# Three of four first normalizations move from ahead of the distance attention into its first units

## What is computed

```
x = x + _L0_attn_ref(_layernorm(x, axis=-1), W_in, b_in, W_out, b_out)

P = X @ W_in + b_in                      # per head: Q, K, V, G of 64 columns each
W = power(1e-4 + cdist(Q, K), -2)        # cdist: root of q2 + k2 - 2 q k
W = W / (1e-4 + sum(W, axis=-1))
H = G * (W @ V)                          # gate times weighted values
return H @ W_out + b_out
```

## Time and profile before

| | us |
|---|---|
| median of 3 runs | 1476.16 (1475.1 to 1477.63) |
| span of the profiled execution | 1475.0 |
| TensorE busy | 1314.3 (89%) |
| VectorE busy | 1067.5 (72%) |
| ScalarE busy | 970.3 (66%) |
| GpSimd busy | 398.6 (27%) |

### The profile page before, as it was taken

One profiled execution on the slowest core, in us unless ns is written; L12 is line 12 of the kernel. 1 busy time (PEld: TensorE's weight loads), 2 busy tenths in 40 slices (PEclk: granted clock), 3 DMA queues, 4 the chain that ended last, 5 costly groups with the idle time before them and its releaser, 6 DMA issues.

```text
span 1475.0 us, 17072 instructions
## 1 busy us (share of the span) xinstructions
PE 1314.3 (89%) x6134; PEld 718.5 (49%) x6134; DVE 1067.5 (72%) x1814; ACT 970.3 (66%) x1264; POOL 398.6 (27%) x262
## 2 busy tenths in 40 slices
PE   6999998999899999567989898899989999986666
PEld 3444454445444544332323232477756767763344
DVE  7788858885888588168988898346548677658895
ACT  4999978997899789334777777445545454433321
POOL 1445533553355335410000000023310000006333
PEclk9999999999999999868999999999989999998887
DMA  8100000000000001000000000000010000000000
GB/s 183 42 1 1 0 1 1 0 1 1 0 1 0 0 1 56 17 1 0 1 0 1 0 1 1 1 1 1 1 54 1 1 1 1 1 1 1 0 8 22
DMA packets 27711, 15.01 MB, mean 10 GB/s; under 512 B 16638, under 2 KB 26476, under 8 KB 27500
## 3 DMA queue, kind: packets, MB, share of 16 engines
q1 hardware_dynamic: 27628, 13.92, 3.5%
HBM read 12.87 MB, written 1.05 MB: 9 GB/s over the span
## 4 chain that ended last, share of the span: by engine, by line
PE 34%; issue 24%; POOL 20%; DVE 18%; ACT 2%; DMA 0%; POOLq 0%; SPq 0%; ACTq 0%; DVEq 0%
POOL ARENA L2134 10%; DVE ARENA L880 9%; POOL ARENA L2139 6%; PE PS L1055 4%; PE PS L729 4%; PE PS L712 4%; PE PS L636 3%; POOL ARENA L2146 3%; PE PS L1063 2%; PE PS L1086 2%; PE PS L1078 2%; PE PS L1067 2%; PE PS L1740 1%; DVE Y L1973 1%; PE PS L1106 1%
## 5 line engine op out<-in xcount | busy, mean ns | idle before, releaser
L1740 PE MATMUL PS<-ARENA 128*128 128x512 f32 x512 | 227.3, 597 | 7.5 <-issue 6.7
L2031 DVE TENSOR_SCALAR ARENA<-PS,ARENA 128x512 f32<-128x512 f32 x256 | 188.1, 748 | 27.6 <-PE PS L1740 9.9
L2134 POOL TENSOR_TENSOR ARENA<-ARENA 128x1024 f32<-128x1024 f32 x64 | 151.3, 2365 | 132.5 <-ACT ARENA L1884 127.5
L880 DVE TENSOR_REDUCE ARENA<-PS 128x2 f32<-128x1024 f32 x128 | 146.4, 1214 | 13.3 <-PE PS L604 12.0
L1740 PEld LDWEIGHTS PS<-ARENA 128*128 128x128 f32 x512 | 95.3, 191 | 117.3 <-issue 113.4
L1868 ACT ACTIVATE ARENA<-ARENA 128x2048 f32<-128x2048 f32 x64 | 119.7, 1905 | 47.6 <-DVE ARENA L2031 47.3
L790 ACT ACTIVATE ARENA<-PS 128x1024 f32<-128x1024 f32 x128 | 128.3, 1025 | 32.4 <-PE PS L623 24.6
L1014 POOL TENSOR_TENSOR ARENA<-ARENA 128x512 f32<-128x512 f32 x32 | 40.6, 1270 | 390.5 <-DVE ARENA L994 390.3
L1876 ACT ACTIVATE ARENA<-ARENA,consts_sb 128x2048 f32<-128x2048 f32 x64 | 127.8, 1996 | 0.4
L1749 PE MATMUL PS<-ARENA 128*64 128x512 f32 x512 | 119.8, 611 | 8.1 <-ACT ARENA L1884 8.1
L1884 ACT ACTIVATE ARENA<-ARENA 128x2048 f32<-128x2048 f32 x64 | 118.3, 1897 | 0.0
(11 more groups left out here) (258 smaller groups left out, 2522.6 us busy)
## 6 DMA issues: line engine op xcount, KB each, us to landing
ARENA<-in_window_bias_dram SPq DMA_DIRECT2D x1, 1536.0 KB, 6.7
WKVG<-in_L_attn_W_in_dram SPq DMA_DIRECT2D x3, 448.0 KB, 6.9
X<-in_x_dram SPq DMA_DIRECT2D x4, 256.0 KB, 5.5
W<-in_L_ffn_w_dram SPq DMA_DIRECT2D x1, 1024.0 KB
out_dram<-X SPq DMA_DIRECT2D x4, 256.0 KB, 2.3
WQ<-in_L_attn_W_in_dram SPq DMA_DIRECT2D x2, 448.0 KB, 8.0
BV<-in_L_attn_b_in_dram SPq DMA_DIRECT2D x1, 512.0 KB, 6.3
Wout<-in_L_attn_W_out_dram SPq DMA_DIRECT2D x1, 512.0 KB, 5.1
```

Of the source, the lines that this page charges most:

```text
L880: dve.tensor_reduce(NMX[:, w % 2, t, 2 * jp:2 * jp + 2], bank(("cS", w, i)), AX.X, ALU.max, negate=True).then_inc(sem("c_max"), 1)
L1740: done(pe.matmul(o, SK[:, hd, kt * P:(kt + 1) * P], MQ[:, hd, :], start=True, stop=True), ("S", u, c))
L2031: dve.tensor_scalar(D[:, u % 2, hd, kt, :], bank(("S", u, c)), K2[:, u % 2, kt, hd:hd + 1], 1e-30, ALU.add, ALU.max).then_inc(sem("guarded ...
L2134: pool.tensor_tensor(WPAIR, D[:, u % 2, hd, 0:2], D[:, u % 2, hd, 2:4], ALU.add).then_inc(sem("w_paired"), 1)
```

## The change

Ahead of the loop only batch 0 is normalized, transposed and copied out. In the loop, `stats(0, u+1)` on VectorE and `rstd(0, u+1)` on ScalarE come in unit `u` (0 to 2); `normalize(0, u)` on VectorE, `ln_turn(0, u)` on TensorE and `xt_out(0, u)` on ScalarE in unit `u` (1 to 3). On VectorE they stand behind the key norms of the unit, on TensorE between its key norms and the next unit's scores, on ScalarE behind the exponentials. GpSimd adds the output bias to batch `u` behind `sum_weights(u)` in units 0 to 3, and no longer waits for its own four additions. The order in which PSUM banks are handed out changes accordingly.

```
 def psum_jobs():
-    jobs = [(("ln", 0, b), 1, [("xt_ready", b + 1)]) for b in range(B)]
+    jobs = [(("ln", 0, 0), 1, [("xt_ready", 1)])]
...
             jobs += project_queries(u + 1) + key_norms(u + 1)
+        if 1 <= u < B:
+            jobs += [(("ln", 0, u), 1, [("xt_ready", u + 1)])]
...
-            for b in range(B):
-                ln_turn(0, b)
+            ln_turn(0, 0)
...
                     key_norms(u + 1)
+                if 1 <= u < B:
+                    ln_turn(0, u)
...
-            for b in range(B):
-                rstd(0, b)
-            for b in range(B):
-                xt_out(0, b)
+            rstd(0, 0)
+            xt_out(0, 0)
...
                 weights(u)
+                if u + 1 < B:
+                    rstd(0, u + 1)
+                if 1 <= u < B:
+                    xt_out(0, u)
...
-            layernorm(0)
+            stats(0, 0)
+            normalize(0, 0)
...
                     key_norms(u + 1)
+                if u + 1 < B:
+                    stats(0, u + 1)
+                if 1 <= u < B:
+                    normalize(0, u)
...
-            for b in range(B):
+            def add_bias(b):
                 pool.wait_ge(sem("ln_y"), b + 1)
                 pool.tensor_tensor(X[:, b], X[:, b], Bout[:].unsqueeze(1).to_broadcast([P, QT, P]),
                                    ALU.add).then_inc(sem("x_biased"), 1)
-            pool.wait_ge(sem("x_biased"), B)
...
                 sum_weights(u)
+                if u < B:
+                    add_bias(u)
```

More of the change, by code:

```diff
@@ L1975, in normalize @@
                 ins.then_inc(sem("ln_y"), 1)
-            def layernorm(k):
-                for b in range(B):
[L1979 to L1982, removed]
             def evacuate_keys(u):
```

## The result

The changed kernel takes 1484.38 us (median of 4 runs, 1482.98 to 1484.99); the kernel before took 1475.63 beside it (1474.66 to 1477.63). The ratio is 1.0055 with a 95% interval of 1.004 to 1.0069: slower by 0.55%, 8.75 us in the medians (1483.4 was forecast, as 7.2 us on top of 1476.16). The profiled executions have spans of 1483.2 and 1475.0.

The account below looks back on a forecast made before the run. TensorE was taken as the loop's bound, without slack; head -4.3, waits 3.64 + 3.64 + 2.44 and clock +1.8 gave +7.2 us on 1476.16, so 1483.4 us. The 8-in-10 range was 1478.0 to 1488.0.

Parts of the forecast that it names:

- Head, -4.3: Before the loop: first scores at 19.2 instead of 23.49, BV's landing the last wait; gain 4.3 us, at least 3.5.
- Weights of the other heads stay covered: After the first scores: remaining weights land at 24.6, TensorE asks at 26.1, so that wait stays covered by 1.5 us.
- The wait in the loop, 3.64 + 3.64 + 2.44 = 9.7: Units 1 to 3: TensorE's transposes wait for VectorE's late normalization, costing 3.64, 3.64 and 2.44 us.
- The clock, +1.8: TensorE's scores after new idle time in units 1 and 2: one clock fall, 1.8 us, bounds 0 and 3.6.
- rival C: VectorE's loop work comes early enough to hide the wait: 1473.2, or 1472.4 without the earlier clock fall; chance 0.08.
- Sum: Whole kernel: -4.3 + 3.64 + 3.64 + 2.44 + 1.8 = +7.2 us, giving 1483.4 us, 0.5% slower.
- Nothing given back: Loop after the wait: TensorE has no slack, so none of the 9.7 us is recovered later.
- ScalarE and GpSimd at no cost: Loop: their added activations, copies and bias additions cost nothing; at most 3.3 us for ScalarE, 1.24 for GpSimd.
- A (port): Units 1 and 2: normalization's end blocked by GpSimd's addition on the shared port, 2.4 to 4.7 us more; chance 0.13.
- B: Loop: ScalarE is the true bound, partly hiding TensorE's new wait; 1475.2, or 1480 with half that wait; chance 0.14.
- D: Start: something else lands late, so the head gains nothing; +11.5 us, 1487.7; chance 0.03.
- The range of the forecast: Whole kernel: the forecast with its clock and head bounds, from 1480.8 to 1486 us, chance 0.62.

Follow-up runs that it names:

- e1_early: Changed kernel, but VectorE does the in-loop normalizations and statistics ahead of the evacuation of queries: 1474.57 us, 0.9992 of the kernel before.
- e2_clock: Changed kernel, but TensorE fills its wait ahead of the three in-loop turns with matmuls whose result is overwritten: 1481.56 us, 1.0037 of the kernel before.
- e7_before_bv: Kernel before, but VectorE waits for the value bias BV only ahead of the evacuation of values: 1477.1 us, ratio 1.0004.
- e5_early_bv: Changed kernel, but VectorE normalizes and takes statistics ahead of evacuating queries, and waits for BV only ahead of the values: 1472.09 us, 0.9966 of the kernel before.
- e3_stats_ahead: Changed kernel, but VectorE's statistics of batches 1 to 3 go back ahead of the loop: 1479.95 us, 1.0027 of the kernel before.

## Why the prediction was right

Forecast 1483.4, measured 1484.4; as a change, +7.2 forecast and +8.75 measured, since the kernel before took 1475.63 beside it and not 1476.16. The mechanism was the forecast one, a wait of TensorE for VectorE's late normalization; the closeness of the total is in part luck, as the terms show. The steps against the profile:

- **Head, -4.3: measured -3.5.** The last wait was BV, as put. It landed 6.9 us after its issue at 7.80 and not 6.3, so VectorE began at 14.79 in place of 14.0; the 5.2 from there to the first scores held (19.98 - 14.79). In e1_early and e2_clock it began at 14.26 and 14.36, for BV was issued earlier (7.44, 7.59) and landed 6.7 later. Over the ten profiles this load took 6.3 to 7.3 us, so the 4.3 was never sure, and the -3.5 lies at the edge of the bounds. The least that I named was 3.5, but for another cause, the slow projections; they took 3.16 for the queries and ended in time.
- **Weights of the other heads stay covered:** held, keys of unit 1 follow the scores at 26.95 without idle time.
- **The wait in the loop, 3.64 + 3.64 + 2.44 = 9.7: measured 9.9.** Take the time from where the scores would start (the last key norm is issued 0.89 after the first) to the turn, and 0.44 for the turn. Unit 1: 55.19 - 51.47 = 3.72. Unit 2: 78.17 - 75.16 = 3.01. Unit 3: 98.73 - 96.89 = 1.84. With three turns of 0.44 to 0.50, 9.9. Each of the three was off, by +0.5, -0.2 and -0.1. In unit 1 VectorE's gated output waited 0.84 for GpSimd's gates, that is for ScalarE, which was busy 21.25 of 21.42 there:

```profile
51.53 0.69 DVE L2036 TENSOR_TENSOR ARENA<-PS,ARENA 128x512 f32<-128x512 f32 x1 [0.84 <-POOL ARENA L2149]
```

Two things make up the 0.84. In e7_before_bv, where TensorE also got ahead by the clock fall it escaped but ScalarE has no added work, the same wait is 0.41. The other 0.43 comes from ScalarE's two small activations, which stand from 39.97 to 40.49 ahead of its next table load: that load starts 5.84 us after the unit's scores, against 5.41 in e7_before_bv. In e2_clock, where the clock did fall over unit 1's scores, VectorE doesn't wait and TensorE's wait from the last key norm to the turn is 3.0 (52.74 to 55.76).
- **The clock, +1.8: measured +2.7.** Falls in both idle spells: 2.33 over the scores of unit 2, 1.09 over those of unit 3, 0.47 on each of two turns, 4.4 in all; and the fall of before over unit 1's scores was absent, -1.7. I had counted one fall for two spells. That the one of before could be absent, which the same idle spell of 2.35 gives or doesn't give, is named in rival C but left out of the sum.
- **Sum:** -3.5 + 9.9 + 2.7 = 9.1, as the first scores of unit 31 show. Two terms were off by 0.8 and 0.9 the same way, and 0.9 of chance behind the loop took one of them back in the profile.
- **Nothing given back:** held, as units 4 and on last 16.72.
- **ScalarE and GpSimd at no cost:** failed by the 0.43 of unit 1, which is ScalarE's; where the clock fell over that unit's scores (e2_clock) it doesn't show. In units 2 and 3 TensorE comes late enough for the work to be hidden (their waits are 0.2 and 0.1 under the forecast). In e5_early_bv, where TensorE isn't late, ScalarE's copy costs 0.12 and 0.23 in two units, as far as the rows show. GpSimd's additions show no cost in the rows.
- **Rivals.** A (port) didn't occur: the fourth operation began 0.47 ahead of GpSimd, where I had reckoned 0.3. It would have cost twice what I said or more; a range up to 1488 would not have held it whole. B and C fell with e1_early and the distances of 20 to 23 us; C is what e1_early builds, at 1474.6, and its 1473.2 missed by 1.4, about the one clock fall more (1.7) in that profile. Its second number is a slip: 1473.2 - 1.8 is 1471.4, not 1472.4. D fell with the head's -3.5.
- **The range of the forecast:** its lower end, 1480.8, is 0.8 under what the bounds give. With the full gain of 4.3 and no fall it is 1483.4 - 1.8 = 1481.6.

## What to carry to other kernels

Work taken from ahead of a loop is hidden only if, on every engine that it crosses, it stands where that engine waits anyway: here 2.3 us on VectorE cost TensorE a wait of 3.0 to 3.7 a unit as last in the queue, ahead of what TensorE asks for next, and none in front of a wait for TensorE's own projections. Ask for each moved step which instruction of the busiest engine it is queued in front of, and what the idle time then does to the clock. And after a head is shortened, look for the next wait: one that was 4 us too early to matter (BV) had become the last.

## What the runs showed of the hardware

- The same idle spell of TensorE lowers the clock in one execution and not in the next. Over the ten profiles: spells of 3.08 us in the attention loop were followed by a fall in 22 of 30, those of 2.34 to 2.39 in 5 of 9, the ten of 2.00 to 2.06 and the five of 1.68 never. Those of 3.56 were followed by a fall in 2 of 2, those of 2.85 in 1 of 2. A fall cost 1.0 to 2.4 us over the scores that followed it, in five of eleven cases 1.7. The Trainium skill, page "TensorE: Matmul & The Clock Gate", section "What's actually happening", has the point of change vary with where the matmuls fall; these counts fit it.
- In units 10, 18 and 26 such a fall costs little or nothing: the scores of unit 11 start 12.56 us after the spell with it (233.56 to 246.12, after) and 12.57 without (224.46 to 237.03, before), and behind the spell TensorE still waits before these scores (0.38 with the fall, 2.01 without). Where the low clock lasted longer (granted 0.70 over the next 10 us) they start 13.3 us after it (e3_stats_ahead: 228.29 to 241.62), and two units on 0.4 to 0.5 is left of the delay. A fall is paid in full only where TensorE is the bound.
- Four VectorE operations of 0.27 us each took 1.08 us when they ended 0.13 us ahead of GpSimd's addition, and 6.19 us when they began 0.11 us behind its start.
